# Degree one-hots of a two-layer graph kernel: every fourth group made by ScalarE as Relu(1 - distance), the others by VectorE as before

## The reference, cut to what matters

```python
# layer 0: GCN, twice, then x = layernorm(x + sigmoid(h))
deg  = segment_sum(ew, dst)                 # ew = edge weights, and 1 for each self loop
dinv = where(deg > 0, rsqrt(deg), 0)
out  = segment_sum((x @ W)[src] * (dinv[src] * ew * dinv[dst])[:, None], dst) + b
# layer 1: attention over incoming edges, then x = layernorm(x + relu(agg + z @ loop_w))
e     = leaky_relu(zs @ a0 + zd @ a1 + rh @ a2)
alpha = softmax of e over the edges of one dst
agg   = segment_sum(alpha * (zs + rh), dst)
```

## Time and profile before

| | us |
|---|---|
| median of three runs | 3388.99 (3383.53 to 3392.19) |
| span of the profiled execution | 2442.5 |
| so, around the span | 946.5 |
| GpSimd busy, share of the span | 1770.9 (73%) |
| TensorE matmul busy | 1839.8 (75%) |
| VectorE busy | 1772.0 (73%) |
| ScalarE busy | 1049.6 (43%) |

### The profile page before, as it was taken

How to read it: one execution, slowest core, us unless ns; L and a number is a source line. 1 busy time by engine, 2 the same in 40 slices (tenths; PEclk the granted TensorE clock), 3 DMA queues, 4 the chain that set the end, 5 groups by cost and what they waited for, 6 DMA issues and landing times.

```text
span 2442.5 us, 40269 instructions
## 1 busy us (share of the span) xinstructions
PE 1839.8 (75%) x13148; PEld 1626.2 (67%) x13148; DVE 1772.0 (73%) x7010; ACT 1049.6 (43%) x1686; POOL 1770.9 (73%) x1813
## 2 busy tenths in 40 slices
PE   5777668898889687788888783146889788668966
PEld 4656667777778566677777673045778677658866
DVE  7998878888788446676677564178776976586686
ACT  0010012433234135676867666612565268326821
POOL 7777777777775377777777775777777777777771
PEclk9567889999999889899988886567889899879988
DMA  5224222222222423444444433764445555555550
GB/s 142 60 79 134 64 67 74 77 82 78 69 83 64 116 70 100 112 119 126 134 122 118 117 107 92 179 180 134 131 127 150 148 140 132 139 145 134 138 136 20
DMA packets 273634, 270.98 MB, mean 111 GB/s; under 512 B 43718, under 2 KB 218973, under 8 KB 273406
## 3 DMA queue, kind: packets, MB, share of 16 engines
q1 hardware_dynamic: 202366, 142.27, 20.3%
q0 software_dynamic: 57664, 119.62, 19.6%
q10 hardware_dynamic: 13392, 6.46, 0.9%
HBM read 254.63 MB, written 13.96 MB: 110 GB/s over the span
## 4 chain that ended last, share of the span: by engine, by line
POOL 28%; DVE 24%; PE 22%; issue 14%; DMA 7%; ACT 3%; SPq 2%; ACTq 0%; POOLq 0%; DVEq 0%
POOL ring L694 28%; PE ps L829 6%; DVE SR L1535 5%; DVE SR L1572 5%; PE ps L881 5%; DMA ring<-h_d,srcC 2%; PE ps L856 2%; DMA ring<-x_d,srcC 2%; PE ps L869 2%; DMA U<-dlo_d 2%; PE ps L831 2%; DVE U L1612 1%; DVE U L1673 1%; PE ps L843 1%; DVE SR L1645 1%
## 5 line engine op out<-in xcount | busy, mean ns | idle before, releaser
L694 POOL DMA_INDIRECT ring<-x_d,srcC x1132 | 1129.8, 998 | 367.0 <-issue 347.9
L829 PE MATMUL ps<-SR,ring 128*128 128x128 f32 x3604 | 628.9, 308 | 90.8 <-DMA ring<-h_d,srcC 38.1
L694 POOL DMA_INDIRECT ring<-h_d,srcC x526 | 499.7, 950 | 208.1 <-issue 201.7
L829 PEld LDWEIGHTS ps<-SR,ring 128*128 128x128 f32 x3604 | 552.1, 221 | 112.4 <-issue 74.0
L1645 DVE TENSOR_SCALAR SR<-iota_r,cols 128x288 f32<-128x288 f32 x686 | 342.1, 562 | 150.0 <-PE ps L881 150.0
L881 PE MATMUL ps<-SR 128*128 128x288 f32 x1372 | 362.0, 416 | 0.0
L831 PE MATMUL ps<-SR 128*128 128x128 f32 x1564 | 315.0, 296 | 6.0 <-DVE SR L1572 6.0
L881 PEld LDWEIGHTS ps<-SR 128*128 128x128 f32 x1372 | 260.4, 196 | 67.9 <-issue 2.8
L1186 ACT COPY SR<-ps 128x512 f32<-128x512 f32 (+1 forms) x182 | 99.3, 559 | 398.2 <-PE ps L869 398.1
L1572 DVE TENSOR_SCALAR SR<-iota,rankC,ewC 128x128 f32<-128x128 f32 x972 | 264.3, 363 | 1.4 <-DVE U L1776 0.3
L831 PEld LDWEIGHTS ps<-SR 128*128 128x128 f32 x1564 | 258.1, 213 | 6.3 <-issue 6.1
(11 more groups left out here) (286 smaller groups left out, 2578.3 us busy)
## 6 DMA issues: line engine op xcount, KB each, us to landing
SR<-in_edge_attr_dram SPq DMA_DIRECT2D x97, 512.0 KB, 4.3
U<-dlo_d SPq DMA_DIRECT2D x98, 256.0 KB
SR<-low_d SPq DMA_DIRECT2D x84, 256.0 KB
ring<-x_d,srcC POOLq DMA_INDIRECT x1132
ring<-h_d,srcC POOLq DMA_INDIRECT x526
ring<-in_edge_attr_dram SPq DMA_DIRECT2D x12, 512.0 KB
U<-lo_d SPq DMA_DIRECT2D x18, 256.0 KB
ring<-low_d SPq DMA_DIRECT2D x36, 128.0 KB
```

The costliest lines, as they stand in the source:

```text
L694: pool.indirect_dma_start(ring[:, ring_at(p, h if p < 2 else q), k, 0:width], None, (x if p == 0 and h < R0 else table)[:, :], bass.Indire ...
L829: last = nc.tensor.matmul(ps[(p * NA + k) % 2][:, at], ring[:, ring_at(p, h), j, 0:D], S[:, gg % NS, j, :], start=False, stop=stop)
```

## The change

The groups q with q % 4 = 1 (1, 5, up to 97: 25 groups, 198 tiles) get their degree one-hots from ScalarE: eight activations Abs(rank - iota), one per tile, then one activation Relu(1 - that) over the whole group, in place, behind a wait on the last Abs. VectorE makes the other 73 groups (584 tiles) as before. Both lists write the same ring `SH`. TensorE waits for the one or the other semaphore. ScalarE's copy of row k is put before the first ScalarE group q that is at least CLOSE[k] + 3. `ones` (the Relu's bias) is set earlier. Two semaphores of `weights()` become one.

```diff
+DEG_ACT = [q for q in range(G) if q % 4 == 1]
+DEG_DVE = [q for q in range(G) if q % 4 != 1]
...
-            pe.wait_ge(s("awT_copied"), 1)
+            pe.wait_ge(s("vectors_made"), 1)
...
-            pe.wait_ge(s("v_made"), 1)
+            pe.wait_ge(s("vectors_made"), 2)
...
             for q in range(G):
-                pe.wait_ge(s("deg_onehot"), q + 1)
+                if q in DEG_ACT:
+                    pe.wait_ge(s("deg_onehot_act"), 2 * DEG_ACT.index(q) + 2)
+                else:
+                    pe.wait_ge(s("deg_onehot"), DEG_DVE.index(q) + 1)
...
         @block.scalar
         def _(act):
-            for k in range(NK):
+            def evacuate_deg(k):
                 act.wait_ge(s("deg_summed"), CLOSE[k] + 1)
                 if k >= 2:
                     act.wait_ge(s("deg_cols"), k - 1)
                 nc.scalar.copy(deg3[:, k % 2, :], ps[6 + k % 2][0:3, :]).then_inc(s("deg_evac"), 1)
+
+            act.wait_ge(s("cols_copied"), 3)
+            for i, q in enumerate(DEG_ACT):
+                for k in range(NK):
+                    if q - 4 < CLOSE[k] + 3 <= q:
+                        evacuate_deg(k)
+                if q >= ND:
+                    act.wait_ge(s("deg_summed"), q - ND + 1)
+                for j, t in enumerate(tiles(q)):
+                    last = nc.scalar.activation(SH[:, q % ND, j, :], iota_h[:, :], ACT.Abs, bias=rankC[:, t:t + 1], scale=-1.0)
+                last.then_inc(s("deg_onehot_act"), 1)
+                act.wait_ge(s("deg_onehot_act"), 2 * i + 1)
+                n = len(tiles(q))
+                nc.scalar.activation(SH[:, q % ND, 0:n, :], SH[:, q % ND, 0:n, :], ACT.Relu, bias=ones[:, 0:1], scale=-1.0).then_inc(s("deg_onehot_act"), 1)
+            for k in range(NK):
+                if CLOSE[k] + 3 > DEG_ACT[-1]:
+                    evacuate_deg(k)
...
             v.tensor_copy(iota_h[:, :], iota_i[:, 0:P])
+            v.memset(ones[:, :], 1.0)
...
-            for q in range(G):
+            for q in DEG_DVE:
                 if q >= ND:
                     dve.wait_ge(s("deg_summed"), q - ND + 1)
                 for j, t in enumerate(tiles(q)):
```

More of the change, by code:

```diff
@@ L1477, in _ @@
             v.memset(zero_h[:, :], 0.0)
-            v.memset(ones[:, :], 1.0)
             v.memset(ones_h[:, :], 1.0)
@@ L1501, in weights @@
                 v.tensor_copy(a1B, awT[:, 1:2].broadcast_to([P, P]))
-                v.tensor_copy(a2B, awT[:, 2:3].broadcast_to([P, P])).then_inc(s("awT_copied"), 1)
+                v.tensor_copy(a2B, awT[:, 2:3].broadcast_to([P, P])).then_inc(s("vectors_made"), 1)
                 dve.wait_ge(s("wprod"), 2)
@@ L1505, in weights @@
                 v.tensor_copy(v1B[:, :], ps[5][:, P:2 * P])
-                v.tensor_copy(v2B[:, :], ps[5][:, 2 * P:3 * P]).then_inc(s("v_made"), 1)
+                v.tensor_copy(v2B[:, :], ps[5][:, 2 * P:3 * P]).then_inc(s("vectors_made"), 1)
             def find_odd():
```

## The result

The change takes 3364.3 us (median of five runs, 3342.46 to 3375.97) against 3388.99 for the kernel before (3383.53 to 3394.20): ratio 0.992, interval 0.9892 to 0.9948. So it is faster by 24.7 us, 0.8%. The forecast was 3361, and its range holds the result.

A forecast was written before the change was run, and what follows sets the result against it. GpSimd's gathers and waits pace the kernel, with consumers lagging through pass 0; the degree stage, paced by VectorE, ends 29 us earlier, 28 is passed on: 3389 - 28 = 3361 us, range 3353 to 3377.

The forecast's parts named there:

- The 946.5 us outside I leave as they are: Final sum: measured time outside the profile's span stays unchanged, so 3389 - 28 = 3361 us.
- 198 x 0.1675 = 33.2 us: Degree stage: one-hot time leaving VectorE, putting its last one-hot at 136.4 instead of 169.6 us; the most the stage can gain.
- ScalarE's group at 3.5 to 3.6 us: Degree stage: ScalarE's price for one group, eight Abs at 0.298 us, a wait of 0.1 and a Relu of 1.05.
- The upper bound (4.3): Degree stage: ScalarE's group would cost 4.3 us if consecutive Abs don't overlap, at 0.39 us each.
- The mixture: Degree stage: TensorE partly at half, partly at full clock; a round of 8.4 us, end near 141, 29 us earlier.
- GpSimd itself comes 3.7 us earlier: Pass 0's change of table: GpSimd's wait of 4.04 us falls to its usual 0.30, so later gathers come earlier.
- The bound at group 29: Pass 0, where sums are closest behind gathers (30.0 us): at most 27 to 33.7 us can be passed on, taken as 31.
- What was passed on: From stage end through pass 0 to the end: 28 us of the stage's 29, about 1 us lost at group 29.
- The first: Rival: ScalarE or the round through it paces the degree stage; gain 18 to 27, 3362 to 3371 us; chance 0.30 with the second.
- The second: Rival: TensorE stays at half rate in the degree stage; end 147, 3366 us; chance 0.30 together with the first.
- The third: Rival: gain swallowed, GpSimd is the bound with 3.7 us left, 3385 us, or consumers lose their lead in pass 0; chance 0.07.
- The fourth: Rival: ScalarE loads a table at each function change, rounds of 14.2 us, stage 33 us later, 3422 us; chance 0.05.

The follow-up runs named there:

- chip C: One of four chips used for the follow-up runs; the kernel before takes 2438.29 us on it.
- e9_after_again: The changed kernel unchanged, on the chip where the kernel before takes 2438.29 us: 2410.01 us, 0.9888 of before.
- chip D: Another of the four chips; the kernel before takes 2443.05 us on it.
- e6_no_scalar: Changed kernel with ScalarE making no one-hots; TensorE reuses those of the group before, so degrees come out wrong: 2409.43 us, against 2410.01 for the change.
- e5_half: Changed kernel with every second group on ScalarE instead of every fourth, copies placed likewise: 3463.69 us, 1.0121 of the kernel before.
- e12_after: The changed kernel unchanged, on the chip where the kernel before takes 2443.05 us: 2407.96 us, ratio 0.986.
- e4_after_held: Changed kernel with GpSimd gathering nothing until the degree stage is over: 3427.72 us, 1.0012 of the kernel before.
- e1_before: The kernel before the change, unchanged, run again for its trace: 3386.27 us, span 3390.8 us.
- after: The first profiled execution of the changed kernel, unchanged, on a slower chip: 3342.46 us, span 3340.6 us.
- e7_copy_later: Changed kernel with each copy of a finished row one ScalarE group later in ScalarE's order: 2408.04 us, against 2410.01 for the change.
- e2_after: The changed kernel unchanged, run again for its trace: 3366.19 us, 0.9924 of the kernel before.
- e8_find_early: Changed kernel with `find_odd` behind VectorE's group 2 instead of 32: 2410.37 us, against 2410.01 for the change.
- e10_find_early: Changed kernel with `find_odd` behind VectorE's group 2 instead of 32, repeated on another chip: 2410.93 us, against 2443.05 for the kernel before.
- e3_before_held: Kernel before with GpSimd gathering nothing until the degree stage is over: 3457.81 us, 1.0102 of the kernel before.

## Why the prediction was right, and where it wasn't

**The failed step** is in the sum: "The 946.5 us outside I leave as they are". Span and time of an execution differ by less than 2 us in every run that has both, so 2442.5 and 3389 are executions of different pace, and the profile that I read is not one of the runs that I was to forecast. The arithmetic put a gain of 28 us on the wrong picture of the rest, and that the sum 3361 fits a slower chip is luck. What it should have raised: 28% of the time outside the span is no launch cost that any row accounts for. A forecast made in span alone, 2414.5, can be held against chip C: there the change takes 2410.01 and its span is 2405.9.

**Step by step, where the rows apply** (e9_after_again against the rows):

| | forecast | before | measured |
|---|---|---|---|
| VectorE's last one-hot | 136.4 | 169.6 | 135.9 |
| last degree matmul | 141 | 170.1 | 137.0 |
| first sum | 160 | 188.8 | 156.8 |
| GpSimd's wait before pass 1 | 24 | 48.05 | 20.4 |
| start of pass 1 | 799 | 826.6 | 797.1 |
| wait before pass 2 | 16.1 | 16.11 | 11.3 |
| lag at the end of pass 0 | 18 | 42 | 14.4 |
| gain in time | 28 | | 28.3, and 35.1 on chip D |

- "198 x 0.1675 = 33.2 us" off VectorE: its one-hots in the chain are 192 in 32.17 and 376 in 63.05 us, 167.6 ns each, and its last is out at 135.9, 33.7 us earlier. Right, and it is the whole gain of the stage (33.1).
- ScalarE's group at 3.5 to 3.6 us: from 89.17 to 92.70 it is 3.53, its Abs at a step of 0.30. Right, and free, as e6_no_scalar shows. The upper bound (4.3) wasn't needed. The Trainium skill's rule ("ScalarE: Activation LUTs", "Rules for kernel authors") that relu, min, max and add belong on VectorE is stated per element. The prediction held its "up to about 3 times" against 3.6 and 1.34 us a group, but there ScalarE makes two passes (Abs, then Relu) where VectorE makes one, so the rows give the price of this work and don't test that figure. As advice the rule fails for a share that fits beside VectorE and holds for e5_half, where ScalarE is the pace.
- The mixture is the mis-sized term: "a round of 8.4 us and an end near 141". From 81.18 to 129.52 six rounds pass, 8.06 us each, and that is VectorE's own 48 x 0.1676 = 8.04; the end is 137.0, and 138.2 in e12_after. (The 7.8 of e4_after_held is VectorE's pace too: there, with no gathers beside it, a one-hot takes 0.163.) TensorE, which was to add its share, stays under that pace. Its mean clock was 0.50 in the earlier trace rows, and in the same stretch of e9_after_again, the first line here, 0.84 (0.73 in e12_after); from 30 to 60 us it is 1.00. The third line is of the kernel before, just ahead of the stretch of the earlier trace rows.

```profile
51.30:102.50 51.20, 33.63 (x454) 26.83 (x452) 50.67 (x260) 38.81 (x100) 39.19 (x40) 0.84 0.24 61
30.00:60.00 30.00, 24.01 (x324) 19.67 (x323) 30.00 (x181) 20.59 (x54) 22.84 (x24) 1.00 0.37 100
```
```profile
30.60:47.90 17.30, 15.33 (x135) 12.30 (x135) 17.30 (x105) 0.57 (x1) 13.31 (x14) 1.00 0.46 128
```

  TensorE takes in 454 matmuls there in 33.63 us where before it took 339 in 38.17. What raised the clock isn't shown. Denser work went with it in this pair and in the held one, but no rule comes of that: before fell from 1.00 to 0.50 though TensorE had been busy 15.33 of 17.30 us and 2.08 of the 3.40 that follow, and in e1_before and after the clock is 1.00 from 60 to 95 us with TensorE busy about 3 of 35. The page "TensorE: Matmul & The Clock Gate" of the Trainium skill (Part 1) makes the half rate a default that sustained activity releases, and the prediction put the end by it nearer 137. The trace agrees on the end and on the higher mean clock, not on those stretches; and it is VectorE that sets 137.
- "GpSimd itself comes 3.7 us earlier" was wrong: its wait of 4.04 is gone, but it starts on `x1_d` at 195.15 instead of 192.68. Its 144 gathers from x are busy 145.5 us instead of 139.4; why isn't settled; they now run on for 58 us behind the degree stage, beside the store and the first sums, where before it was 18 us. The bound at group 29 was nearly reached: its sum begins at 327.31, 1.7 us behind the end of its last gather (325.61), where 4 were forecast and 30.0 were before. But L834 waits for no gather in pass 0, and its waits for one-hots are 15.6 us against 22.4.
- What was passed on: 33.1 us at the stage's end, 32.0 at the first sum, 29.5 at the start of pass 1. So about 3.6 are lost on the way, where I had put 1. Behind that the gain grows again, which the forecast didn't have: 34.2 us at the start of pass 2, whose wait shrank from 16.11 to 11.26 instead of staying, and 36.6 by span. The profile of before (2442.5) is some 6 us above the spans of before on chip C (its time there is 2438.29), so the 28.3 us of that chip, close to 28, are one of two results; chip D's 35.1 lies outside the forecast gain of 25 to 32. What makes up the rest isn't settled.
- In the reading of the bound, the 593.1 us called issue between the gathers hold the waits of 48.05 and 16.11 us; without them they are 529.

**The rivals.** The first (ScalarE paces) is out at this share on the quicker chips by e6_no_scalar and e7_copy_later, and true at twice the share. The second (half rate) is out by the clock and the ends of e4_after_held and e9_after_again. The third (swallowed) is out by the 28.3 and 35.1 us. The fourth (table loads): Abs, Relu and Copy follow each other in every timeline without one.

**On the chips of the measurement** the gain of 20.8 to 24.7 us has another make-up. The mechanism of the forecast is only seen there with GpSimd held (32.2 us in the stage, 30.1 in the time). Undisturbed, one-hots advance almost only in GpSimd's pauses, the change shortens the two in the stage (by 10.0 and 10.3 us in after, 4.8 and 9.9 in e2_after), and the pause before pass 1, from which the forecast drew all its gain, doesn't shrink. In the last stretch ScalarE is even the pace: VectorE is done at 278.2 us, and TensorE goes on until 290.0. TensorE is busy for most of that, but what it waits for is ScalarE (3.6 us between 262 and 291), which has no pause from 267.6 on, at 7.5 us a round.

```profile
286.82 1.11 PE L787 MATMUL ps<-SR,cols 128*3 128x128 bf16 x17 [0.99 <-ACT SR L1171]
```

So for these chips the forecast of 28 is near the 24.7 by luck: both start from the 33 us of one-hots, but go different ways, and the steps behind the stage don't hold here. Open is how much of the 24.7 is find_odd's earlier end and how much the shorter last stretch; e8_find_early and e10_find_early were to tell and fell on the other kind of chip.

## What to carry to other kernels

Before you build on a profile, hold its span against the time of its own execution, and against the times you are to forecast. Here a profile and its own time differed by less than 2 us; a gap of 946 meant that the profile was of something else, and a constant added to it was a guess. Work can be moved to an engine that is almost three times slower at it without cost, as long as its sum per round stays under the pace that remains: ScalarE's 7.5 us (two groups of 3.53 and a copy) beside VectorE's 7.8 to 8.06 did, 14.5 didn't. Where a stage is freed of one engine's load, ask for each wait later on whether it is really the one that shrinks.

## What the runs showed of the hardware that I hadn't expected

One program takes 2438, 2443, 3387 or 3424 us on four chips. On the slower ones, in the degree stage, VectorE and TensorE start one instruction per 1.40 us each while GpSimd issues indirect DMAs at its usual 1.25 us. They are back at full pace 9.5 us after its last gather ends (97.6 to 107.1 in after), with the DMA engines 3% busy meanwhile: the slow pace outlasts GpSimd's instructions and nearly all of the transfers. The two instruction queues carry 110 and 103 packets in the profile of after and in that of e9_after_again alike, so it isn't that more code is loaded.

ScalarE is hit as well. Between 150 and 235 us of e1_before it executes nothing, though the row that closes with group 40 had been summed at 163.0. Its copy of that row comes 5.7 us after the last gather, and TensorE stands for it:

```profile
244.62 0.57 ACT L1152 COPY U<-ps 3x512 f32<-3x512 f32 x1 [107.51 <-remote]
245.25 1.86 PE L771 MATMUL ps<-ones,U 3*128 3x1 f32 x8 [66.17 <-ACT U L1152]
```

In e3_before_held and e4_after_held, with no gather running, none of this is seen in the stage. What makes the other engines wait on these chips isn't settled by any run here; only that in this stage it comes with the gathers and goes without them is.
